# Two streams of attention and expert layers: the next attention's keys and norm are made earlier

## The reference

```
x = x + t(g_xattn[0]) * A0(LN(x), ctx)          # 16 heads of 8; q, k, v through relu; no output projection
x = x + t(g_ffn[0])   * F0(LN(x))               # SELU gate net, 8 SELU experts 128-512-128, top 2
x = x + t(g_xattn[1]) * A1(LN(x), ctx, adj, mask[b])  # 16 heads; biases, adj added to scores, a mask per sequence
x = x + t(g_ffn[1])   * F1(LN(x))               # bit layer: rmsnorm, int8 activations, ternary weights, gelu
x = x + t(g_xattn[2]) * A2(LN(x), ctx, mask)    # 16 heads; one mask for all
x = x + t(g_ffn[2])   * F2(LN(x))               # SiLU experts with low-rank terms, 8, top 2
x = x + t(g_xattn[3]) * A3(LN(x), ctx)          # "class attention": one head of 64, output tiled
x = x + t(g_ffn[3])   * F3(LN(x))               # per head top 2 of 16 small gelu experts
# A:  softmax(q k^T / sqrt(dh) [+ adj, masked]) v, heads joined [, output projection]
# F1: y = q8(rmsnorm(x)) w1 + b1;  out = q8(rmsnorm(gelu(y))) w2 + b2
```

## Time and profile before

| what | us |
|---|---|
| runs of the kernel before | 1931.27, 1930.8, 1916.35 (median 1930.8) |
| the profiled execution | 1916.38 |
| its span, first to last instruction | 1914.6 |
| mean granted TensorE clock, share of full | 0.841 |
| TensorE products busy | 1348.0 (70%) |
| TensorE weight loads busy (beside products) | 666.6 (35%) |
| VectorE busy | 987.2 (52%) |
| ScalarE busy | 751.5 (39%) |
| GpSimd busy | 402.5 (21%) |

### The profile page before, as it was taken

One profiled execution on the slowest core, in us unless ns is written; L12 is line 12 of the kernel. 1 busy time (PEld: TensorE's weight loads), 2 busy tenths in 40 slices (PEclk: granted clock), 3 DMA queues, 4 the chain that ended last, 5 costly groups with the idle time before them and its releaser, 6 DMA issues.

```text
span 1914.6 us, 21114 instructions
## 1 busy us (share of the span) xinstructions
PE 1348.0 (70%) x7836; PEld 666.6 (35%) x7836; DVE 987.2 (52%) x2268; ACT 751.5 (39%) x1102; POOL 402.5 (21%) x462
## 2 busy tenths in 40 slices
PE   3456978865647697867477797886473869886756
PEld 2223544441212334531222455444121233453211
DVE  3347546656563453462552664666656445346252
ACT  0034643522324143337266463353232413433636
POOL 4306020025030200015332601001503020001424
PEclk9988999987559898969578898999755989896969
DMA  8204112112020200012420311300202020001221
GB/s 269 37 7 77 51 48 63 34 39 40 1 33 2 34 1 1 1 28 88 66 73 23 83 45 38 74 23 12 45 1 33 1 33 2 1 1 17 94 61 61
DMA packets 49221, 78.57 MB, mean 41 GB/s; under 512 B 15056, under 2 KB 34272, under 8 KB 48496
## 3 DMA queue, kind: packets, MB, share of 16 engines
q0 software_dynamic: 18752, 34.69, 7.7%
q1 hardware_dynamic: 25616, 25.25, 6.3%
q10 hardware_dynamic: 4752, 17.30, 2.9%
HBM read 52.63 MB, written 2.10 MB: 29 GB/s over the span
## 4 chain that ended last, share of the span: by engine, by line
PE 53%; DVE 18%; issue 12%; ACT 9%; DMA 4%; POOL 3%; SPq 1%; POOLq 0%; ACTq 0%; DVEq 0%
PE ps L705 5%; PE ps L587 5%; PE ps L721 5%; PE ps L538 5%; DVE nm L1205 4%; PE ps L809 4%; PE ps L863 3%; PE ps L543 3%; PE ps L811 3%; PE ps L852 3%; PE ps L799 3%; ACT hT L1075 3%; DVE ps L1221 2%; PE ps L570 2%; DVE hT L1403 1%
## 5 line engine op out<-in xcount | busy, mean ns | idle before, releaser
L341 POOL TENSOR_TENSOR rstd<-vare,mhalf 128x4 f32<-128x4 f32 x40 | 42.4, 1063 | 1191.2 <-DVE vare L1145 1131.2
L1205 DVE TENSOR_REDUCE nm<-ps 128x4 f32<-128x1024 f32 x192 | 231.8, 1222 | 113.9 <-PE ps L543 113.1
L965 ACT ACTIVATE pT<-ps 128x1024 f32<-128x1024 f32 x192 | 194.2, 1026 | 166.9 <-DVE ps L1221 103.8
L1075 ACT ACTIVATE hT<-ps,w_l_b 128x512 f32<-128x512 f32 x256 | 158.2, 684 | 91.6 <-PE ps L852 89.8
L705 PEld LDWEIGHTS ps<-l_ring,hT 128*128 128x128 f32 x1152 | 154.1, 206 | 79.7 <-issue 78.0
L705 PE MATMUL ps<-l_ring,hT 128*128 128x128 f32 x1152 | 157.8, 291 | 26.6 <-DVE acc L1343 25.1
L1403 DVE SCALAR_TENSOR_TENSOR hT<-ex,rl 128x512 f32<-128x512 f32 x144 | 104.4, 730 | 123.2 <-ACT rl L1014 99.2
L721 PE MATMUL ps<-xT,l_ring 128*128 128x512 f32 x288 | 164.9, 664 | 4.0 <-ACT rl L1014 4.0
L1013 ACT ACTIVATE ex<-ps,l_exp_bias 128x512 f32<-128x512 f32 x144 | 99.2, 689 | 172.3 <-PE ps L721 171.8
L852 PE MATMUL ps<-ex,w1s 96*128 96x512 bf16 x256 | 101.5, 438 | 75.2 <-ACT hT L1075 49.8
L587 PE MATMUL ps<-pT,vA 128*32 128x256 f32 x1536 | 122.8, 447 | 33.0 <-ACT oT L945 31.3
(11 more groups left out here) (256 smaller groups left out, 2097.7 us busy)
## 6 DMA issues: line engine op xcount, KB each, us to landing
l_ring<-in_l_wio ACTq DMA_DIRECT2D x33, 512.0 KB, 3.8
gate<-f_gate_rows POOLq DMA_DIRECT2D x64, 256.0 KB, 3.7
kS<-kp POOLq DMA_DIRECT2D x144, 64.0 KB, 3.5
qS<-qp SPq DMA_DIRECT2D x144, 64.0 KB
w_l_w<-in_l_w SPq DMA_DIRECT2D x3, 1024.0 KB
ex<-gate POOLq DMA_DIRECT2D x24, 128.0 KB, 5.3
pT<-in_l_wo SPq DMA_DIRECT2D x1, 2048.0 KB
m<-in_mask_q POOLq DMA_DIRECT2D x4, 512.0 KB, 6.2
```

What stands on the lines that cost most here:

```text
L965: act.activation(pT[:, v % NPB, :], scores, ACT.Exp).then_inc(sem("p_ready"), 1)
L1075: act.activation(hid3[:, n % 8, :], bank(5 + n % 2), ACT.Gelu, bias=W["l3_b1"][:, ep:ep + 1])\
L1205: dve.tensor_reduce(nm[:, 2 * b:2 * b + 2, :, j].rearrange("p t g -> p g t"), ps[:, sl:sl + 2, :].rearrange("p g (t k) -> p g t k", t=2), ...
```

## The change

- *Keys of the next attention.* A new helper `ahead` names the attention that follows in the order, if it is not a class attention. Its keys are projected while the current attention runs: TensorE's product at due time 8.0 (14.0 in a class attention) into PSUM bank 4, ScalarE's copy at 9.5 (15.0), GpSimd's split (`key_parts`) at 23.0, and GpSimd's twelve stacking transfers (`key_stack`) at END - 1, behind the last score product of the current attention. Only A(0,0) makes its own. With attention 0 the context transposes and their copy move along; SP loads the contexts earlier.
- *Norm of the next attention.* F(·,0), F(·,1) and F(·,2) end with the norm for the attention that follows in their own stream: VectorE behind the residual sum (due times `OVER`), GpSimd's root, TensorE's transposes into bank 6, ScalarE's copy. The next expert layer's first product waits for that copy (`start_experts`). Attentions 1, 2 and 3 begin with query and value products at once. Attention 0 norms at its own start as before.
- *Order in the attention.* The query split goes ahead of the value copy on VectorE, at due time 3.0; SP's stack at 4.0; `FIRST_SLOT` falls from 25 to 18, so slots, shift, closing norm and END all move seven units ahead in the merge with the expert layer.
- *Bit layer.* Its due times move back, and the second quantisation is cut into five pieces 2.6 units apart.
- *Attention 1.* The two bias tiles no longer share one buffer (the query's is made in place of the mask), and GpSimd makes them in earlier stages.

The diff, cut to its core:

```diff
-FIRST_SLOT, SLOT = 25.0, 1.3
+FIRST_SLOT, SLOT = 18.0, 1.3
...
+        m1f = m1[:].rearrange("p t k -> p (t k)").bitcast(f32).rearrange("p (t k) -> p t k", t=NT)
...
+        def ahead(job):
+            jobs = [at for at, _ in order if at is not None]
+            n = jobs.index(job) + 1
+            return jobs[n] if n < len(jobs) and jobs[n][1] < 3 else None
...
-            def keys(m):
+            def key_parts(m):
+                if m:
+                    pool.wait_ge(sem("k_stack"), 16 * HP * NSEG * m)
                 pool.wait_ge(*upto("kf", m, 1))
                 step(pool.tensor_copy(kp[:, 0, :], kf[:]))
                 step(pool.tensor_tensor(kf[:], kf[:], kp[:, 0, :], ALU.subtract))
                 step(pool.tensor_copy(kp[:, 1, :], kf[:]))
-                step(pool.tensor_tensor(kp[:, 2, :], kf[:], kp[:, 1, :], ALU.subtract))
+                pool.tensor_tensor(kp[:, 2, :], kf[:], kp[:, 1, :], ALU.subtract).then_inc(sem("kp"), 1)
+            def key_stack(m):
+                pool.wait_ge(*upto("kp", m, 1))
                 if m:
                     pool.wait_ge(*upto("s2", m - 1, 2 * NK))
                 for n, part in enumerate(Y_PARTS):
...
+                after = ahead((i, a))
                 yield 1.0
-                if a == 3:
-                    root(i)
-                else:
+                if a < 3:
                     attention_over(pool, (i, a))
-                    root(i)
+                    if a == 0:
+                        root(i)
+                if place(i, a) == 0:
                     yield 3.0
-                    keys(place(i, a))
-                    if i % 2 and a == 0:
-                        yield 10.0
-                        mask_in(i - 1, 0)
-                        yield 14.0
-                        bias(i - 1, 0)
-                        mask_in(i - 1, 1)
-                        yield 24.0
-                        query_bias(i - 1)
-                        yield 32.0
-                        bias(i - 1, 1)
-                    if a == 1 and i % 2 == 0:
-                        yield 10.0
-                        mask_in(i + 1, 0)
-                    if a == 1 and i % 2:
-                        yield 5.0
-                        bias(i, 0)
-                        mask_in(i, 1)
-                        yield 12.0
-                        query_bias(i)
-                        yield 22.0
-                        bias(i, 1)
+                    key_parts(0)
+                    key_stack(0)
+                if a == 0 and i % 2:
+                    yield 12.0
+                    mask_in(i - 1, 0)
+                if a == 1 and i % 2 == 0:
+                    yield 16.0
+                    mask_in(i + 1, 0)
+                if a == 1 and i % 2:
+                    yield 16.0
+                    bias(i, 1)
+                if after is not None:
+                    yield 23.0
+                    key_parts(place(*after))
+                if a == 0 and i % 2:
+                    yield 26.0
+                    bias(i - 1, 0)
+                    yield 34.0
+                    query_bias(i - 1)
+                    mask_in(i - 1, 1)
+                    yield 48.0
+                    bias(i - 1, 1)
+                if a == 1 and i % 2 == 0:
+                    yield 34.0
+                    bias(i + 1, 0)
+                    yield END - 12.0
+                    query_bias(i + 1)
+                    mask_in(i + 1, 1)
+                if after is not None:
+                    yield END - 1.0
+                    key_stack(place(*after))
                 yield END + 8.0
                 root(i)
...
                 if n == 1:
-                    root(i)
-                    yield 16.0
+                    for at in BIT_ROOTS:
+                        yield at
+                        root(i)
+                if n < 3:
+                    yield OVER[n] + 1.0
                     root(i)
                 if n == 3:
...
+            def keys(i, a, to):
                 if a == 0:
                     pe.wait_ge(sem("ctx_loaded"), 16 * (i + 1))
                     for t in range(NT):
-                        last = pe.transpose(bank(3)[:, t * P:(t + 1) * P], cr[:, t, :], W["ident"][:])
+                        last = pe.transpose(bank(to)[:, t * P:(t + 1) * P], cr[:, t, :], W["ident"][:])
                     last.then_inc(sem("cT_ps"), 1)
                     pe.wait_ge(sem("cT_ready"), i + 1)
+                pe.matmul(bank(to), W[f"l{a}_wk"][:], cT[i % 2][:], start=True, stop=True).then_inc(sem("k_ps"), 1)
             def attention(i, a):
                 s, m, L = i % 2, place(i, a), f"l{a}_"
+                after = ahead((i, a))
                 yield 0.0
                 start_attention(i, a)
-                pe.matmul(bank(0), W[L + "wk"][:], cT[s][:], start=True, stop=True).then_inc(sem("k_ps"), 1)
+                if m == 0:
+                    keys(i, a, 3)
+                    pe.wait_ge(*upto("kf", 0, 1))
+                if a == 0:
+                    yield 6.0
+                    norm_T(i, LN_OF_ATT[a])
+                    yield 7.5
+                pe.wait_ge(*of("xT_ready", i, 7, n_T(LN_OF_ATT[a])))
+                pe.matmul(bank(3), W[L + "wq"][:], xT[s][:], start=True, stop=True).then_inc(sem("q_ps"), 1)
                 for t in range(NT):
                     last = pe.matmul(bank(1)[:, t * P:(t + 1) * P], cT[s][:, t * P:(t + 1) * P], W[L + "wv"][:],
                                      start=True, stop=True)
                 last.then_inc(sem("v_ps"), 1)
-                yield 6.0
-                norm_T(i, LN_OF_ATT[a])
-                yield 7.5
-                pe.wait_ge(*of("xT_ready", i, 7, n_T(LN_OF_ATT[a])))
-                pe.matmul(bank(3), W[L + "wq"][:], xT[s][:], start=True, stop=True).then_inc(sem("q_ps"), 1)
+                if after is not None:
+                    yield 8.0
+                    keys(*after, 4)
...
                         pe.wait_ge(*upto("vf", m, 1))
+                        if after is not None:
+                            pe.wait_ge(*upto("kf", place(*after), 1))
...
+            def start_experts(i, n):
+                experts_over(pe, (i, n))
+                last = before((i, n), 1)
+                if last is not None and last[1] < 3:
+                    pe.wait_ge(*of("xT_ready", last[0], 7, n_T(LN_OF_ATT[last[1] + 1])))
+            def next_T(i, n):
+                norm_T(i, LN_OF_ATT[n + 1], 6)
...
+                yield OVER[0] + 3.0
+                next_T(i, 0)
...
+                if after is not None:
+                    yield 9.5
+                    act.wait_ge(*upto("kp", m, 1))
+                    keys(*after, 4)
...
-                statistics(i, src)
-                yield 4.0
+                    statistics(i, xn[s])
+                    yield 4.0
+                    dve.wait_ge(sem(f"x_copied_{s}"), i // 2 + 1)
+                    normal(i, xn[s])
+                    yield 10.0
+                else:
+                    yield 3.0
+                dve.wait_ge(*upto("qf", m, 1))
+                step(dve.tensor_copy(qp[:, 0, :], qf[:]))
+                step(dve.tensor_tensor(rest_a, qf[:], qp[:, 0, :], ALU.subtract))
+                step(dve.tensor_copy(qp[:, 1, :], rest_a))
+                dve.tensor_tensor(qp[:, 2, :], rest_a, qp[:, 1, :], ALU.subtract).then_inc(sem("qp"), 1)
+                yield 10.5 if a == 0 else 5.0
...
-            def quantise(i, src, dst, F, n):
+            def quantise(i, src, dst, F, n, at, gap, done):
                 s = i % 2
                 dve.tensor_scalar(vare[s][:], cols[:, 0, :], 1.0 / F, EPS, ALU.mult, ALU.add)\
                    .then_inc(sem(f"var_ready_{s}"), 1)
+                yield at + gap
                 root(i)
                 step(dve.tensor_tensor(cols[:, 2, :], cols[:, 1, :], rstd[s][:], ALU.mult))
                 step(dve.tensor_scalar(cols[:, 3, :], cols[:, 2, :], 1e-5, None, ALU.max))
...
                 step(dve.scalar_tensor_tensor(cols[:, 5, :], cols[:, 4, :], 127.0, rstd[s][:], ALU.mult, ALU.mult))
                 step(dve.tensor_scalar(cols[:, 6, :], cols[:, 3, :], wmean[:, n:n + 1], 1.0 / 127.0,
                                        ALU.mult, ALU.mult))
+                yield at + 2 * gap
                 for t in range(NT):
                     ins = dve.tensor_scalar(src[:, t, :], src[:, t, :], cols[:, 5, t:t + 1], -128.0,
                                             ALU.mult, ALU.max)
                 step(ins)
+                yield at + 3 * gap
                 step(dve.tensor_scalar(src, src, 127.0, MAGIC, ALU.min, ALU.add))
-                return dve.tensor_scalar(dst, src, -MAGIC, None, ALU.add)
+                yield at + 4 * gap
+                dve.tensor_scalar(dst, src, -MAGIC, None, ALU.add).then_inc(sem(done), 1)
+            def next_norm(i, n):
+                statistics(i, x[i % 2])
+                yield OVER[n] + 2.0
+                normal(i, x[i % 2])
...
```

(18 more changed lines are left out.)

143 lines of the change are left out of this document (74 added, 69 removed).

## The result

The changed kernel took 1938.4 us (median of 13 runs, 1933.4 to 1943.7), the kernel before 1928.2 (13 runs, 1916.4 to 1932.0). The ratio is 1.007 with a 95% interval of 1.005 to 1.009: 0.7% slower, less than the 1% named as the limit. The forecast was 1902, faster.

A forecast was written before the change was run, and what follows sets the result against it. Bound: stage by stage, TensorE standing for the norm, query, split and transfer chain, worst over the bit layer. Terms -24 + 1 - 8 + 14.4 - 2.5 = -19.1 took 1916.4 to 1897, or 1912 by the median; forecast 1902, range 1868 to 1940.

The forecast's parts named there:

- the price of the expert slots that lose their place ahead of the first score: Attention 1 over expert layer 0: three fewer slots ahead, 2.1 us each, leave 6.2 us; stage net +0.5 each.
- The same term in A(·,0): Attention 0 over expert layer 0, turns 1 and 3: shorter opening and earlier closing norm, 4 us gained each, -8 together.
- The closing norm: Attention over expert layer 0: moved seven units ahead, expert slots fill its wait, about 2.5 us gained per stage.
- GpSimd beside VectorE: Key splits on GpSimd beside VectorE work: bounds 0 and 2.2 us per attention, 0 and 24 in all; taken as 0.
- the 1921 of one hold for each split: Whole kernel if each GpSimd key split blocked one VectorE operation: sum +5 instead of -19, time 1921 us.
- F(·,2): Stages over expert layer 2: exposed next norm costs 5.0 us; attention 2 +2.2 each, class attention +5.0 each, +14.4 together.
- F(·,3): Class attention over expert layer 3: query product first, keys in turn 1, closing norm earlier; +3.5 and +1 us.
- A(2,0): Attention 0 of turn 2 over expert layer 3: expert batch 7 to 9 us sooner, scores up to 12; stage -7.
- The bit stages: Four stages over the bit layer: earlier query and scores, attention 1 gains 4 us each, attention 2 gains 8; sum -24.
- the keys' own work I cost at nothing: Key product, copy, split and transfers hide in waits at no cost; uncovered, each would cost about 2 + 0.7 + 7 us.
- The one with the other sign: Rival, chance 0.18: norm exposed at eight ends behind expert layers 0 and 2, query stack no sooner; +27, 1943 us.
- The opening is worth all of it: Rival, chance 0.17: quantisation pieces fit between maxima; bit stages -45, attention 0 of turn 2 -12; 1871 us.

The follow-up runs named there:

- the runs at 18.4 and 25: Changed kernel with attention's score slots over expert layer 0 at due time 18.4 or 25 instead of 18: 1914.1 us (one run) and 1865.5 us (median of 4).
- the kernel whose shift is not stretched: Changed kernel with GpSimd's bias for the next turn's query started five exponentials before the last in attention 1 over expert layer 0: 1924.9 us, ratio 0.997.
- The run with own keys: Changed kernel with slots at 25 over expert layer 0 and each attention making its keys at its own start: 1919.0 us, ratio 0.997 to the kernel before.

## Why the prediction was wrong, step by step

- **What failed: the price of the expert slots that lose their place ahead of the first score.** The step was "the scores now stand behind nine slots, not twelve; at 2.1 each that is 6.2 us of work still to do". 2.1 is the spacing of slots in the opening. By the runs at 18.4 and 25 three slots cost 10.9 to 12.2 in each of the four stages (3.6 to 4.1 each, with the top-2 work that moves along), 45.5 in all; the sum had 6.2 in each of two stages, 12.4. It priced the slot by the place it left, not by the place it went to.
- **The same term in A(·,0) was left out,** and this is the larger part: 23.4 of the 45.5 us. I counted the shorter opening (4 each) and the closing norm, and no slots given up. The first score did come earlier by more than I said (34.7 against 43.9 behind the residual in A(1,0), 28.9 against 34.3 in A(3,0)), and all of it was spent again.
- **Phase was not in the sum at all.** A due time of 18 instead of 18.4 cost 23 us over four stages, 13.5 of it against the kernel whose shift is not stretched, both by one run. The order written out by hand decides which of two ready operations goes first, and the wait lines of before can't show it for another order.
- **The miss of 44.4 over F(·,0), added up.** The slots took 33.1 more than charged, and 23.4 lie between 18 and 18.4; against that, with the slots at 25 the four stages are 31.5 shorter than before, where the sum without its slot term had 19.4, so 12.1 better. What the change does to these stages apart from the merge order was underrated, not overrated.
- **The closing norm gives nothing.** "Less about 2.5 because the attention's closing norm moves seven units ahead" was taken twice over F(·,0). TensorE's waits for VectorE's `acc` come to 8.6 us in A(1,0) in both kernels (the longest 3.9, before 4.2) and in A(0,1) to 6.1, before 4.8: the slots behind the closing norm filled no wait.
- **GpSimd beside VectorE: bounded, and small in sum.** Summed over the whole trace, VectorE operations that ran while GpSimd computed took some 32 us more than the median of their form before, and some 35 after: 3, where 0 was taken and 24 left to the range. But one of the holds hit the shift of A(0,1), by 2.8, and one that of A(2,1), by 1.9. The Trainium skill ("SBUF — State Buffer", Who interferes with whom) has both sides of it: the four hT activations, with two SBUF inputs each, were held, and the maxima (1.22) never grew; that the tensor_scalar of the shift was held as well, with one tensor read, is more than the sentence on two inputs covers, but the section lists tensor_scalar among the operations that can take the shared pair. The key splits do hold VectorE up in their new place (four activations of A(0,1) that begin at 291.74 took 5.68 us together, where one takes 0.69), but holds of the old order went away; the 1921 of one hold for each split was too much.
- **F(·,2): right in A(·,3), wrong in A(·,2).** The exposed norm cost 4.7 and 3.1 in A(·,3) over F(·,2), forecast 5, and the run without it gave back 5.3 and 4.9. A(·,2) got 5.4 shorter where 2.2 longer was forecast: its first score came 7.7 earlier (38.3 to 30.6 behind the residual), the attention behind it took as long as before (83.2, 83.1), so the slot given up cost nothing that shows here, and the end of the stage gave back 2.3, not 5.0. Time line at the end of A(0,3) (answers to the earlier trace rows): from the end of the last expert sum to the end of the last copied transpose 10.7 us (825.80 to 836.45), forecast 11.0, and 5.9 before:

```profile
824.68 1.12 DVE L1416 SCALAR_TENSOR_TENSOR acc<-ps,gw,acc 128x128 f32<-128x128 f32 x4 [2.15 <-PE ps L858]
...
834.70 1.11 PE L527 MATMUL ps<-w_ident,xn 128*128 128x128 f32 x4 [4.10 <-DVE xn L1229]
...
835.85 0.60 ACT L968 ACTIVATE xT<-ps 128x512 f32<-128x512 f32 x1 [4.62 <-PE ps L527]
```

- **F(·,3): open.** A(1,3) and A(3,3) took 6.3 and 6.7 more, forecast +3.5 and +1. But in the run of the kernel before with the slots at 18 over F(·,0), whose code and order in these two stages are those of the kernel before, they took 97.0 and 97.5, at a granted clock of 0.74 and 0.73 instead of 0.80 and 0.79; against it the changed kernel's are 1.4 and 1.7 longer. By the run that moved the class norm back, that norm costs 4.6 in A(3,3) and nothing in A(1,3). So the 13 us can't be put down to the change as they stand, and how much of them it made stays open. A(1,3) in the kernel before, then in that run (columns as above):

```profile
822.50:914.60 92.10, 63.84 (x278) 23.77 (x278) 41.09 (x172) 51.14 (x84) 33.60 (x40) 0.80 0.22 61
...
850.30:947.30 97.00, 69.55 (x281) 24.71 (x282) 41.01 (x171) 51.42 (x84) 33.47 (x40) 0.74 0.22 57
```

- **A(2,0): right in the stage, larger at the opening.** Counted from the stage's start (929.27; 914.62 before) the expert's stack is issued at 4.8 us (20.4 before), its first product runs at 13.9 (943.16 on the time line; 32.6 before) and the scores at 27.1 (956.36; 40.8 before; answers to the earlier trace rows). The product comes 18.7 sooner, where 7 to 9 were said, the scores 13.7, where up to 12 were said; the stage -9.2, forecast -7. The run with own keys gives 7.2 of it to the keys.

```profile
934.08 3.22 POOL L462 DMA_DIRECT2D ex<-gate  x6 [2.12 <-DVEq L1575]
...
956.36 0.61 PE L582 MATMUL ps<-kS,qS 48*128 48x256 bf16 x4 [7.23 <-issue]
```

- **The bit stages: right in sum (-21 against -24), wrong in the split.** A(·,1) gained 12.4 where 8 was said, A(·,2) 8.7 where 16. What the keys do there was mis-stated: "the keys' own work I cost at nothing" holds only since they are made ahead; without that the gain of an early query in these stages shrinks to 0 to 4 us each.
- **The rivals.** The one with the other sign named the exposed norm and 1943; the time came near it, the mechanism did not: the first scores of A(0,1) and A(2,1) came 29.5 and 29.1 us behind the residual, where it asked for a stack later than 32, and the two kernels without that norm behind F(·,0) got at most 3.5 us back in a stage there. "The opening is worth all of it" is nearer in number to what the change can do: with only the merge order put right, the median is 1865, below its 1871. But 31.5 us of that lie over F(·,0), which that rival did not name; the four bit stages had 30.

## What to carry to other kernels

When a hand-written order moves one stream ahead, count the other stream's slots that lose a place in a wait, and price each by what it costs where it lands, not by its spacing where it was: here 3.6 to 4.1 us against 2.1. Fill the wait for a transfer until the engine no longer stands there, and not beyond; after every change that shortens or lengthens the wait, set the due times anew, stage by stage, in whole pitches. Of two transfers that are awaited together, moving one ahead is worth what the other allows.

## What the runs showed of the hardware that I had not expected

The stands cost twice. In A(1,0) and A(0,1) TensorE did the same work in 106.53 and 124.59 us at a granted clock of 0.88, and in 101.92 and 117.62 us at 0.93 and 0.94 once three more slots lay in the wait: 11.6 us of busy time in two stages, on top of the idle time. A part can be the execution: the same instructions of A(1,3) ran at 0.80 and at 0.74 in two executions, as shown above. Behind the stretched shift of A(0,1) the granted clock averaged 0.64 of full speed over five microseconds, between its levels of 1.2 and 2.4 GHz and nearer to the lower, while TensorE was busy 4.14 of 5.00:

```profile
365.00:370.00 5.00, 4.14 (x18) 2.56 (x18) 1.38 (x2) 2.29 (x3) 0.00 (x0) 0.64 0.01 3
```

And two stacks of twelve transfers in flight together land late. In the run with own keys the key stack's last issue in A(0,2) ended at 546.57, 2.1 us behind the query stack's last, and the stack landed 10.7 us later. Where the query stack was issued only after it, in A(1,0), A(2,0) and A(3,0) of the same run, the same twelve transfers landed 3.1 to 3.5 us behind their last issue; in the six stages where the two overlapped it was 9.6 to 11.5, and in A(·,2) over F(·,2), where they met for less than 2 us, 5.2 and 5.4. From issue to landing a key transfer took 3.9 to 11.3 us in A(0,2), 6.6 in the median, against 3.5 in the median of the whole kernel before.
